# A convolution stage on TensorE: high and low activation parts in one stationary operand, input weights 128 columns wide

## The chip, the cores and the metric

The kernel runs on one core of a Trainium2 chip. The metric is the device time of one execution in microseconds (us). A core has TensorE (PE in the profile, with its weight loads as PEld), VectorE (DVE), ScalarE (ACT), GpSimd (POOL) and SyncE (SP), which here issues nearly all DMAs of the stage under study. The engines run their own queues in order and wait for each other on semaphores.

## The reference

The input x is 16 images of 16 x 16 positions with 192 channels, in float32: 4096 tokens of 192 values. Three layers follow one another. Only the first is touched by the change:

```
xs  = einsum('bhwc,dc->bhwd', x, W1) + b1      # 192 -> 48 channels ("input product")
xs  = gelu(xs)
xs  = |low-pass(xs)|                           # 2-D FFT, mask, inverse FFT, per image and channel
xs  = einsum('bhwd,cd->bhwc', xs, W2) + b2     # 48 -> 192 channels ("output product")
x   = x + xs
```

Then come an attention layer over the 12 heads of each token with a row normalisation ahead of it, and a mixture of 8 experts (top 2) of width 384, each added to x. The result is float32 throughout, and the low-pass is one 256 x 256 matrix over the positions of an image.

## The kernel before, in words

The kernel is four phases, one after the other, each a block of its own that all engines enter and leave together: `conv_phase`, `attention_phase`, `routing_phase`, `expert_phase`. Only `conv_phase` (lines 139 to 436) is touched.

**Tiles.** The 4096 tokens are 32 tiles of 128; four tiles (512 tokens, two images) are one "quad", so there are eight quads. Two slots (`RING` = 2) hold quads in flight; quad number q is 2i + s, in slot s.

**TensorE** does three products for each quad. `in_product` (line 233) takes the transposed x, 192 channels on the partitions in two parts of 128 and 64 (+1 row of ones for the bias), as the stationary operand of 128 tokens, and the 48 columns of W1 as the moving operand, in plain float32: eight products a quad, which the profile shows as 16 matmul instructions (lines 239, 240). `lowpass_product` (line 243) has six: activations split into a high and a low part (`g_hi`, `g_lo`, type float32r), times the 256-wide low-pass matrix, itself split; high x high, high x low and low x high are summed. The two images m of a quad lie at partitions 0 to 63 and 64 to 127, each using 48 rows and one for the bias. `out_product` (line 254) has twelve: for each image m and half h, `yt_hi` x `w2_hi`, `yt_hi` x `w2_lo` and `yt_lo` x `w2_hi`, each on 49 partitions (at 0 or at 64), 192 columns wide. The order on TensorE is written out by hand (lines 268 to 282): in the loop, `in_product(i,0)`, `lowpass_product(i-1,1)`, `out_product(i-1,0)`, `in_product(i,1)`, `lowpass_product(i,0)`, `out_product(i-1,1)`.

**ScalarE** first makes `lp_hi` and `w2_hi` (lines 291 to 295) after five constant loads, and then, per quad, `gelu` (line 297: GELU out of PSUM, and a copy that rounds it to `g_hi`), `magnitude` (line 308: the absolute value twice, into `yt` and rounded into `yt_hi`), and `split` (line 317: rounds one expert's weights, two instructions of 768 columns, waiting for their load).

**VectorE** makes the low parts by subtraction: `g_low` (399), `yt_low` (406), `split` (413, expert weights, `wb_lo`), and `finish` (380: adds the output product to x and takes row statistics).

**GpSimd** makes the other low part of the expert weights (`wa_lo`, line 352) and the four small steps of the row deviation.

**SyncE** issues the loads in one queue, in this order per quad: `load` (the transposed x, after `in_product` of two quads before), `load_rows` (x itself), `load_weights` (line 196: one expert's weights, after `wa_lo` and `wb_lo` of two quads before). So a wait in `load_weights` holds all loads behind it.

Of the kernel before, what the change touches and what calls it, by code (L numbers as in the profile page):

```python
# [138 lines left out]
def conv_phase(nc, xs, shift, rstd, x_tiles, xT, w1, w2, lowpass, wgu, wa_hi, wa_lo, wb_hi, wb_lo, ytab, eye, ident,  # L139
               later):  # L140

    with ExitStack() as stack:
        a = Scope(nc, stack, "conv")
        w1a, w1b = a.sb("w1a", [P, DH]), a.sb("w1b", [CB + 1, DH])
        w2s = a.sb("w2s", [P, C])
# [5 lines left out]
        yt = a.sb("yt", [P, RING, SEQ])  # L151
        yt_hi, yt_lo = a.sb("yt_hi", [P, RING, SEQ], F32R), a.sb("yt_lo", [P, RING, SEQ], F32R)

# [22 lines left out]
        g_lo_done, yt_lo_done = a.sem("g_lo_done"), a.sem("yt_lo_done")  # L176
        g_made = a.sem("g_made")
        pool_turn, dve_turn = a.sem("pool_turn"), a.sem("dve_turn")

        with nc.Block() as block:  # L180
            @block.sync
            def _(sp):
                sp.dma_start(w1a[:], w1[0:P, :]).then_inc(w1_in, 16)
                sp.dma_start(w1b[:], w1[P:C + 1, :]).then_inc(w1_in, 16)

# [19 lines left out]
                load(0, 1)  # L205
                sp.dma_start(lp[:], lowpass.rearrange("(h p) s -> p h s", p=P)).then_inc(consts_in, 16)
                sp.dma_start(w2s[0:DH + 1, :], w2).then_inc(consts_in, 16)
                sp.dma_start(w2s[DP:DP + DH + 1, :], w2).then_inc(consts_in, 16)
# [17 lines left out]
            def _(pe):  # L226
# [6 lines left out]
                def in_product(i, s):  # L233
                    q = quad(i, s)
                    pe.wait_ge(xt_in[s], 32 * i + 32)
                    pe.wait_ge(gelu_done, freed(q))
                    for t in range(QT):
                        at = ps_w1[:, s, t * DH:(t + 1) * DH]
                        nc.tensor.matmul(at, xta[:, s, bass.ts(t, P)], w1a[:], start=True, stop=False)  # L239
                        last = nc.tensor.matmul(at, xtb[:, s, bass.ts(t, P)], w1b[:], start=False, stop=True)  # L240
                    last.then_inc(w1_done, 1)
# [12 lines left out]
                def out_product(i, s):  # L254
                    q = quad(i, s)
                    pe.wait_ge(yt_lo_done, made(q))
                    pe.wait_ge(added, freed(q))
                    for m in range(2):
                        k = slice(DP * m, DP * m + DH + 1)
                        for h in range(2):  # L260
                            at = ps_c[:, s, m, h * C:(h + 1) * C]
                            hi, lo = yt_hi[k, s, bass.ts(h, P)], yt_lo[k, s, bass.ts(h, P)]
                            nc.tensor.matmul(at, hi, w2_hi[k, :], start=True, stop=False)
                            nc.tensor.matmul(at, hi, w2_lo[k, :], start=False, stop=False)
                            last = nc.tensor.matmul(at, lo, w2_hi[k, :], start=False, stop=True)
                    last.then_inc(w2_done, 1)
# [18 lines left out]
            def _(act):  # L285
# [5 lines left out]
                nc.scalar.activation(lp_hi[:], lp[:], ACT.Copy)  # L291
                for k in (0, DP):
                    b = slice(k, k + DH + 1)
                    ins = nc.scalar.activation(w2_hi[b, :], w2s[b, :], ACT.Copy)
                ins.then_inc(const_hi_done, 1)

                def gelu(i, s):
# [4 lines left out]
                    nc.scalar.activation(g[:, s].rearrange("p h m d -> p m h d")[:, :, :, 0:DH],  # L302
                                         ps_w1[:, s, 0:QT * DH].rearrange("p (m h d) -> p m h d", m=2, h=2),
                                         ACT.Gelu).then_inc(g_made, 1)
# [3 lines left out]
                def magnitude(i, s):  # L308
                    q = quad(i, s)
                    act.wait_ge(fft_done, made(q))  # L310
                    act.wait_ge(w2_done, freed(q))
                    act.wait_ge(yt_lo_done, freed(q))
                    for dst in (yt, yt_hi):
                        ins = nc.scalar.activation(dst[:, s, :], ps_f[:, s, 0:SEQ], ACT.Abs, bias=y_bias[:, 0:1])
                    ins.then_inc(abs_done, 1)
# [54 lines left out]
            @block.vector  # L370
            def _(dve):
                nc.vector.memset(xtb[CB:CB + 1, :, :], 1.0).then_inc(bias_row, 1)
                dve.sem_inc(added, RING)
                dve.sem_inc(g_lo_done, RING)
# [18 lines left out]
                nc.vector.tensor_tensor(lp_lo[:], lp[:], lp_hi[:].bitcast(F32), ALU.subtract)  # L393
                for k in (0, DP):
                    b = slice(k, k + DH + 1)
                    ins = nc.vector.tensor_tensor(w2_lo[b, :], w2s[b, :], w2_hi[b, :].bitcast(F32), ALU.subtract)
                ins.then_inc(const_lo_done, 1)

# [7 lines left out]
                def yt_low(i, s):  # L406
                    q = quad(i, s)
                    dve.wait_ge(abs_done, made(q))
                    dve.wait_ge(w2_done, freed(q))
                    nc.vector.tensor_tensor(yt_lo[:, s], yt[:, s], yt_hi[:, s].bitcast(F32),  # L410
                                            ALU.subtract).then_inc(yt_lo_done, 1)

# [975 lines left out]
```

## Time and profile before

| | us |
|---|---|
| median of three runs | 485.05 |
| lowest, highest | 484.86, 489.58 |
| the profiled execution, its own time | 490.49 |
| its span (first to last instruction) | 488.7 |
| TensorE busy in the span | 407.5 (83%) |
| VectorE, ScalarE, GpSimd busy | 273.0, 222.3, 277.1 |
| mean granted TensorE clock that the profile gives | 0.87 |

The convolution stage ends at about 73 us, attention and gate logits take up to about 191 us, routing up to about 232 us, and the experts the rest. Busy time is the time in which an engine has an instruction in it; it tells nothing of how fast the engine is clocked. A timeline row is: start, length, engine, line, operation, what is written and read, the tile's shape, how many instructions were merged in the row, and in brackets how long the engine had stood idle and for whom. The distance between the starts of two rows is the pace of the engine; the length of a matmul is longer, since matmuls overlap.

### The profile page before, as it was taken

Reading aid. Unit: us, or ns where it says so; the run is one execution under the profiler, and the core shown is the slowest. Engines: PE = TensorE matmul, PEld = TensorE weight load, DVE = VectorE, ACT = ScalarE, POOL = GpSimd, SP = SyncE. Lnnn points to the kernel's source line nnn. Section 1 sums busy time; section 2 is a strip of 40 time slices with the busy share of each in tenths; the row PEclk is TensorE's granted clock in tenths of the full one; section 3 lists DMA queues with packets and bytes.
Section 4 is the critical chain, followed back from the end, with each engine's and each line's share of the span. In section 5 each row is a group of like instructions: output and inputs, shape, how many; then the busy total and the mean of one; then the engine's idle time right before and its main releaser. Section 6 shows DMA issues by size and latency. Waiting matters only on the chain.

```text
span 488.7 us, 9018 instructions
## 1 busy us (share of the span) xinstructions
PE 407.5 (83%) x2236; PEld 381.4 (78%) x2237; DVE 273.0 (56%) x716; ACT 222.3 (45%) x513; POOL 277.1 (57%) x297
## 2 busy tenths in 40 slices
PE   5899936886998875175899999999999999999870
PEld 5799925675987674065799999999989989998870
DVE  1266573486677432996356666665555555464540
ACT  3533510435454441084455555555545545555340
POOL 0165560377576540001656787878878788787653
PEclk9999999996595555555799999999999999999895
DMA  7988513003334243100323444444434444444442
GB/s 214 269 202 246 148 14 93 24 1 100 99 101 143 86 122 110 14 0 12 100 40 59 67 71 73 68 68 77 72 63 76 77 60 73 66 75 70 55 42 25
DMA packets 46439, 41.26 MB, mean 84 GB/s; under 512 B 14121, under 2 KB 40524, under 8 KB 46412
## 3 DMA queue, kind: packets, MB, share of 16 engines
q0 software_dynamic: 13824, 16.82, 21.8%
q1 hardware_dynamic: 32588, 24.14, 18.2%
q8 instruction: 10, 0.16, 0.1%
q14 instruction: 17, 0.14, 0.1%
HBM read 25.87 MB, written 15.08 MB: 84 GB/s over the span
## 4 chain that ended last, share of the span: by engine, by line
POOL 20%; issue 15%; DMA 13%; PE 2%; SPq 1%; POOLq 0%; ACT 0%; DVE 0%; ACTq 0%
DMA out<-moe_y,idx_map 13%; POOL moe_xt L1063 10%; POOL out L1071 10%; SPq L1308 1%; DMA moe_xt<-rows,idx_map 1%; POOLq L1056 0%; PE moe_ps_gt L1105 0%; PE moe_ps_x L1096 0%; PE moe_ps_y L1130 0%; PE moe_ps_gt L1106 0%; PE moe_ps_h L1116 0%; PE moe_ps_gt L1107 0%; PE moe_ps_gt L1109 0%; PE moe_ps_u L1105 0%; PE moe_ps_u L1109 0%
## 5 line engine op out<-in xcount | busy, mean ns | idle before, releaser
L1071 POOL DMA_INDIRECT out<-moe_y,idx_map x72 | 114.3, 1587 | 48.0 <-SPq L1319 24.8
L1063 POOL DMA_INDIRECT moe_xt<-rows,idx_map x72 | 71.2, 988 | 58.7 <-issue 58.7
L1206 ACT ACTIVATE moe_yy<-moe_ps_y,moe_xt 128x384 f32<-128x384 f32 x72 | 41.9, 582 | 72.3 <-PE moe_ps_y L1130 72.3
L1130 PE MATMUL moe_ps_y<-wd,moe_h_hi 128*128 x216 | 71.4, 356 | 0.7 <-DVE moe_h_lo L1261 0.5
L1269 DVE TENSOR_TENSOR moe_y<-moe_yy 128x192 f32<-128x192 f32 x72 | 25.9, 359 | 80.2 <-DMA out<-moe_y,idx_map 53.0
L1186 ACT ACTIVATE moe_x_hi<-moe_ps_x 128x256 fp32r<-128x256 f32 x72 | 27.6, 383 | 46.3 <-PE moe_ps_x L1097 46.3
L1130 PEld LDWEIGHTS moe_ps_y<-wd,moe_h_hi 128*128 128x128 f32 x216 | 41.0, 190 | 2.3 <-issue 2.3
L1261 DVE TENSOR_TENSOR moe_h_lo<-moe_ps_h,moe_h_hi 128x384 fp32r<-128x384 f32 x72 | 40.2, 558 | 2.8 <-ACT moe_h_hi L1198 0.5
L1255 DVE TENSOR_TENSOR moe_hid<-moe_ps_u,moe_sg 128x384 f32<-128x384 f32 x72 | 39.5, 549 | 1.2 <-ACT moe_sg L1192 1.2
L1132 PE MATMUL moe_ps_y<-wd,moe_h_lo 128*128 x144 | 36.3, 252 | 0.0
L1116 PE MATMUL moe_ps_h<-eye,moe_hid 128*128 128x128 f32 x216 | 35.8, 275 | 0.0
L1198 ACT ACTIVATE moe_h_hi<-moe_ps_h 128x384 fp32r<-128x384 f32 x72 | 35.4, 492 | 0.7 <-PE moe_ps_h L1116 0.7
L617 PE MATMUL attn_ps_q<-wqa,attn_xa 128*128 128x240 f32 x64 | 27.9, 532 | 9.1 <-ACT attn_xb L649 9.1
L1192 ACT ACTIVATE moe_sg<-moe_ps_gt 128x384 f32<-128x384 f32 x72 | 35.0, 486 | 0.0
L1245 DVE TENSOR_TENSOR moe_x_lo<-moe_ps_x,moe_x_hi 128x128 fp32r<-128x128 f32 x72 | 20.8, 288 | 22.2 <-ACT moe_x_hi L1186 22.0
L1105 PE MATMUL moe_ps_gt<-wa_hi,moe_x_hi 128*128 x72 | 26.5, 368 | 6.5 <-DVE moe_x_hi L1248 6.4
L352 POOL TENSOR_TENSOR wa_lo<-conv_stage,wa_hi 128x768 f32 (+1 forms) x8 | 15.1, 1887 | 28.3 <-ACT wb_hi L320 28.3
L1105 PE MATMUL moe_ps_u<-wa_hi,moe_x_hi 128*128 x72 | 30.9, 429 | 0.0
L617 PEld LDWEIGHTS attn_ps_q<-wqa,attn_xa 128*128 128x128 f32 x64 | 17.2, 283 | 13.9 <-issue 11.7
L1132 PEld LDWEIGHTS moe_ps_y<-wd,moe_h_lo 128*128 128x128 f32 x144 | 27.4, 190 | 0.0
L618 PE MATMUL attn_ps_q<-wqb,attn_xb 65*128 65x240 f32 x64 | 26.6, 510 | 0.0
L239 PE MATMUL conv_ps_w<-conv_w1a,conv_xta 128*128 128x48 f32 x64 | 20.3, 417 | 7.5 <-DMA conv_xtb<-in_xT 7.5
(184 smaller groups left out, 1131.0 us busy)
## 6 DMA issues: line engine op xcount, KB each, us to landing
xs<-in_x SPq DMA_DIRECT2D x8, 384.0 KB, 4.9
conv_stage<-in_wgu SPq DMA_DIRECT2D x8, 384.0 KB, 3.7
conv_stage<-in_wgu SPq DMA_DIRECT2D x16, 192.0 KB, 4.2
rows<-attn_xr SPq DMA_DIRECT2D x8, 384.0 KB, 2.7
out<-xs SPq DMA_DIRECT2D x8, 384.0 KB, 3.4
attn_stage<-in_down SPq DMA_DIRECT2D x8, 288.0 KB, 3.4
conv_xta<-in_xT SPq DMA_DIRECT2D x8, 256.0 KB, 4.1
moe_xt<-rows,idx_map POOLq DMA_INDIRECT x72, 2.8
```

The costliest lines, as they stand in the source:

```text
L617: nc.tensor.matmul(at, xa[:, s, bass.ts(t, P)], wqa[:], start=True, stop=False)
L1063: nc.gpsimd.indirect_dma_start(xt[:, slot, :], None, rows.ap(), bass.IndirectOffsetOnAxis(ap=idx_map[:, j, 0:1], axis=0)).then_inc(gathere ...
L1071: nc.gpsimd.indirect_dma_start(out, bass.IndirectOffsetOnAxis(ap=idx_map[:, j, 1:2], axis=0), y[:, j % YR, :], None, compute_op=ALU.add).t ...
L1105: nc.tensor.matmul(at, x_hi[:, s, 0:P], wa_hi[:, e, w], start=True, stop=False)
L1116: ins = nc.tensor.transpose(ps_h[:, bass.ts(k, P)], hid[:, s, bass.ts(k, P)], eye[:])
L1130: ins = nc.tensor.matmul(both, hi, halves, start=(k == 0), stop=(k == 2))
L1132: nc.tensor.matmul(first, lo, high, start=False, stop=False)
L1192: nc.scalar.activation(sg[:, s, :], ps_g[:, s, 0:HID], ACT.Silu).then_inc(silu_done, 1)
L1198: nc.scalar.activation(h_hi[:, s, :], ps_h[:, 0:HID], ACT.Copy).then_inc(h_hi_done, 1)
L1206: nc.scalar.activation(yy[:, s].rearrange("p h c -> p (h c)"), ps_y[:, s, 0:2 * C], ACT.Copy, scale=xt[:, slot, bass.ds(GC + e, 1)]).then_ ...
L1255: nc.vector.tensor_tensor(hid[:, s, :], ps_u[:, s, 0:HID], sg[:, s, :], ALU.mult).then_inc(hid_done, 1)
L1261: nc.vector.tensor_tensor(h_lo[:, s, :], ps_h[:, 0:HID], h_hi[:, s, :].bitcast(F32), ALU.subtract).then_inc(h_lo_done, 1)
```

## The change

In the input product the weights `w1a`, `w1b` become 128 columns wide, with 80 columns of zeros, so that each matmul moves 128 columns in place of 48 and writes a full 128 columns of PSUM. GELU reads the 48 that count. VectorE fills both tiles with zeros first, and SyncE waits for that (`wide`) before its first load.

In the output product, `yt_hi` and `yt_lo` go into one tile `yt_hl`: for image m, the high part lies on that image's own 64 partitions and the low part on the other 64. With W2's high part on both halves of the partitions, one matmul over 128 partitions gives high x high + low x high, and a second one with W2's low part gives high x low + low x low (a term that was left out before). Twelve matmuls of 49 partitions become eight of 128. ScalarE's magnitude is now three instructions (`yt` on 128 partitions, the high part of each image on 64), and `yt_low` two on 64 partitions. `w2s` is filled with zeros before its load (`w2_filled`), since all 128 partitions are now used; its splits into high and low become one instruction each.

```diff
-        w1a, w1b = a.sb("w1a", [P, DH]), a.sb("w1b", [CB + 1, DH])
+        w1a, w1b = a.sb("w1a", [P, P]), a.sb("w1b", [CB + 1, P])
...
-        yt_hi, yt_lo = a.sb("yt_hi", [P, RING, SEQ], F32R), a.sb("yt_lo", [P, RING, SEQ], F32R)
+        yt_hl = a.sb("yt_hl", [P, RING, 2, SEQ], F32R)
...
             def _(sp):
-                sp.dma_start(w1a[:], w1[0:P, :]).then_inc(w1_in, 16)
-                sp.dma_start(w1b[:], w1[P:C + 1, :]).then_inc(w1_in, 16)
+                sp.wait_ge(wide, 2)
+                sp.dma_start(w1a[:, 0:DH], w1[0:P, :]).then_inc(w1_in, 16)
+                sp.dma_start(w1b[:, 0:DH], w1[P:C + 1, :]).then_inc(w1_in, 16)
...
+                sp.wait_ge(w2_filled, 1)
                 sp.dma_start(w2s[0:DH + 1, :], w2).then_inc(consts_in, 16)
...
-                        at = ps_w1[:, s, t * DH:(t + 1) * DH]
+                        at = ps_w1[:, s, t * P:(t + 1) * P]
...
                     for m in range(2):
-                        k = slice(DP * m, DP * m + DH + 1)
                         for h in range(2):
                             at = ps_c[:, s, m, h * C:(h + 1) * C]
-                            hi, lo = yt_hi[k, s, bass.ts(h, P)], yt_lo[k, s, bass.ts(h, P)]
-                            nc.tensor.matmul(at, hi, w2_hi[k, :], start=True, stop=False)
-                            nc.tensor.matmul(at, hi, w2_lo[k, :], start=False, stop=False)
-                            last = nc.tensor.matmul(at, lo, w2_hi[k, :], start=False, stop=True)
+                            both = yt_hl[:, s, m, bass.ts(h, P)]
+                            nc.tensor.matmul(at, both, w2_hi[:], start=True, stop=False)
+                            last = nc.tensor.matmul(at, both, w2_lo[:], start=False, stop=True)
...
-                for k in (0, DP):
-                    b = slice(k, k + DH + 1)
-                    ins = nc.scalar.activation(w2_hi[b, :], w2s[b, :], ACT.Copy)
-                ins.then_inc(const_hi_done, 1)
+                nc.scalar.activation(w2_hi[:], w2s[:], ACT.Copy).then_inc(const_hi_done, 1)
...
-                    for dst in (yt, yt_hi):
-                        ins = nc.scalar.activation(dst[:, s, :], ps_f[:, s, 0:SEQ], ACT.Abs, bias=y_bias[:, 0:1])
+                    nc.scalar.activation(yt[:, s, :], ps_f[:, s, 0:SEQ], ACT.Abs, bias=y_bias[:, 0:1])
+                    for m in range(2):
+                        b = slice(DP * m, DP * (m + 1))
+                        ins = nc.scalar.activation(yt_hl[b, s, m, :], ps_f[b, s, 0:SEQ], ACT.Abs, bias=y_bias[b, 0:1])
                     ins.then_inc(abs_done, 1)
...
             def _(dve):
+                nc.vector.memset(w1a[:], 0.0).then_inc(wide, 1)
+                nc.vector.memset(w1b[:], 0.0).then_inc(wide, 1)
                 nc.vector.memset(xtb[CB:CB + 1, :, :], 1.0).then_inc(bias_row, 1)
+                nc.vector.memset(w2s[:], 0.0).then_inc(w2_filled, 1)
...
-                    nc.vector.tensor_tensor(yt_lo[:, s], yt[:, s], yt_hi[:, s].bitcast(F32),
-                                            ALU.subtract).then_inc(yt_lo_done, 1)
+                    for m in range(2):
+                        b, o = slice(DP * m, DP * (m + 1)), slice(DP * (1 - m), DP * (2 - m))
+                        ins = nc.vector.tensor_tensor(yt_hl[o, s, m, :], yt[b, s], yt_hl[b, s, m, :].bitcast(F32),
+                                                      ALU.subtract)
+                    ins.then_inc(yt_lo_done, 1)
```

## Rows read from the trace of the kernel before

**Rows 1.** Page, part 2, whole span: granted clock and DMA share in 40 slices.
```profile
PEclk9999999996595555555799999999999999999895
DMA  7988513003334243100323444444434444444442
```

**Rows 2.** Timeline, PE, one quad: start, length, engine, line, operation, count.
```profile
44.96 0.66 PE L239 MATMUL conv_ps_w<-conv_w1a,conv_xta 128*128 128x48 f32 x2
...
48.39 0.56 PE L249 MATMUL conv_ps_f<-conv_lp_hi,conv_g_hi 128*128 128x256 f32 x1
...
49.61 0.41 PE L251 MATMUL conv_ps_f<-conv_lp_hi,conv_g_lo 128*128 128x256 f32 x1
49.95 0.53 PE L263 MATMUL conv_ps_c<-conv_w_hi,conv_yt_hi 49*128 49x192 f32 x1
...
50.50 0.62 PE L263 MATMUL conv_ps_c<-conv_w_hi,conv_yt_hi 49*128 49x192 f32 x2
...
51.68 0.41 PE L265 MATMUL conv_ps_c<-conv_w_hi,conv_yt_lo 49*128 49x192 f32 x1
52.02 0.66 PE L239 MATMUL conv_ps_w<-conv_w1a,conv_xta 128*128 128x48 f32 x2
```

**Rows 3.** Timeline, PE: one kind of instruction (128x128 transpose) at three times.
```profile
85.95 0.42 PE L498 MATMUL attn_ps_b<-eye,attn_xn 128*64 128x128 f32 x1
86.17 0.42 PE L497 MATMUL attn_ps_a<-eye,attn_xn 128*128 128x128 f32 x1
...
103.96 0.27 PE L497 MATMUL attn_ps_a<-eye,attn_xn 128*128 128x128 f32 x1
104.07 0.27 PE L498 MATMUL attn_ps_b<-eye,attn_xn 128*64 128x128 f32 x1
...
129.10 0.42 PE L498 MATMUL attn_ps_rb<-eye,attn_xr 128*64 128x128 f32 x1
```

**Rows 4.** Windows: busy us and count by engine, granted clock, DMA share, GB/s.
```profile
12.00:27.00 15.00, 12.81 (x60) 12.00 (x60) 5.67 (x17) 6.95 (x15) 4.21 (x2) 1.00 1.03 262
27.00:54.00 27.00, 27.00 (x133) 25.43 (x132) 16.10 (x48) 12.20 (x24) 15.58 (x20) 1.00 0.78 213
16.70:52.00 35.30, 35.27 (x170) 33.34 (x170) 18.87 (x55) 15.46 (x31) 18.56 (x21) 1.00 0.86 227
102.30:112.50 10.20, 6.85 (x40) 5.90 (x38) 7.49 (x23) 4.61 (x11) 7.19 (x14) 1.00 0.01 2
112.50:133.00 20.50, 18.40 (x63) 16.00 (x64) 15.70 (x40) 9.65 (x22) 12.29 (x23) 0.50 0.41 119
```

**Rows 5.** Timeline, PE, attention stage: products 240 and 8 columns wide.
```profile
92.24 1.01 PE L617 MATMUL attn_ps_q<-wqa,attn_xa 128*128 128x240 f32 x2
...
103.34 0.57 PE L618 MATMUL attn_ps_q<-wqb,attn_xb 65*128 65x240 f32 x2
...
135.57 0.39 PE L623 MATMUL attn_ps_q<-ga,attn_ra 128*128 128x8 f32 x2
135.89 0.39 PE L624 MATMUL attn_ps_q<-gb,attn_rb 64*128 64x8 f32 x2
```

**Rows 6.** Waits of SP's own queue, 0 to 75 us: total, times, longest.
```profile
SPq L199 <- DVE wb_lo L416: 21.0, 6, 5.1
```

**Rows 7.** Timeline, all engines: start of the kernel, and the second pass.
```profile
0.76 0.40 SPq L183 DMA_DIRECT2D conv_w1a<-in_w  x1
...
1.03 0.91 DVE L372 MEMSET conv_xtb<- 1x1024 f32 x1 [1.03 <-PEq L1380]
...
16.73 0.66 PE L239 MATMUL conv_ps_w<-conv_w1a,conv_xta 128*128 128x48 f32 x2 [1.65 <-DMA conv_xtb<-in_xT]
```

**Rows 8.** Timeline, all engines: splits of one quad; the stage's last instruction.
```profile
43.37 0.47 ACT L314 ACTIVATE conv_yt_hi<-conv_ps_f,conv_y_bias 128x256 fp32r<-128x256 f32 x1
...
43.87 0.43 DVE L410 TENSOR_TENSOR conv_yt_lo<-conv_yt,conv_yt_hi 128x256 fp32r<-128x256 f32 x1 [0.82 <-ACT conv_yt_hi L314]
...
72.54 0.20 POOL L472 TENSOR_TENSOR shift<-conv_minus,rstd 128x4 f32<-128x4 f32 x1 [0.20 <-POOL rstd L467]
```

More of the change, by code:

```diff
@@ L176, in conv_phase @@
         g_lo_done, yt_lo_done = a.sem("g_lo_done"), a.sem("yt_lo_done")
-        g_made = a.sem("g_made")
+        g_made, w2_filled, wide = a.sem("g_made"), a.sem("w2_filled"), a.sem("wide")
         pool_turn, dve_turn = a.sem("pool_turn"), a.sem("dve_turn")
@@ L302, in gelu @@
                     nc.scalar.activation(g[:, s].rearrange("p h m d -> p m h d")[:, :, :, 0:DH],
-                                         ps_w1[:, s, 0:QT * DH].rearrange("p (m h d) -> p m h d", m=2, h=2),
+                                         ps_w1[:, s].rearrange("p (m h d) -> p m h d", m=2, h=2)[:, :, :, 0:DH],
                                          ACT.Gelu).then_inc(g_made, 1)
@@ L393, in _ @@
                 nc.vector.tensor_tensor(lp_lo[:], lp[:], lp_hi[:].bitcast(F32), ALU.subtract)
[L394 to L397, printed above, removed]
+                nc.vector.tensor_tensor(w2_lo[:], w2s[:], w2_hi[:].bitcast(F32),
+                                        ALU.subtract).then_inc(const_lo_done, 1)
                 def g_low(i, s):
```

## The prediction

> **What bounds the kernel now.** I read the page's 40 slices first, then the timeline of one quad, the same instruction at several times to learn the clock, the busy time by stretches, and last the waits of SyncE. In the first slices TensorE is busy without a break and the DMA share is high; the clock digits read 9 throughout the convolution [rows 1]. That digit misleads. A transpose of 128 columns lasts 0.42 us at 85.95, where the page still prints full clock, and 0.27 us at 103.96; it lasts 0.42 us again at 129.10 [rows 3], in a stretch whose granted clock is 0.50 [rows 4]. The spacing is 0.22 us in the first case and 0.11 us in the second [rows 3]. So the printed 1.00 ahead of 102 us is no measurement, and at 85.95 TensorE ran at its lower level, 1.2 GHz.
>
> One quad in the convolution: 16 input matmuls in 48.39 - 44.96 = 3.43 us, 0.214 us each; six low-pass matmuls up to 49.95, 1.56 us; twelve output matmuls up to 52.02, 2.07 us; 7.06 us in all [rows 2]. A slot of 0.214 us is the same for 48 and for 256 moving columns (from 49.61 on, less the gap at the end), and it is the 0.22 us of a transpose at 1.2 GHz: what is paid is the load of 128 stationary columns, at the lower clock. TensorE is busy 35.27 of 35.30 us between 16.7 and 52 [rows 4]. It is the bound there, and DMA is the next one: its share is 1.03 at 262 GB/s in 12 to 27 us, when the second pass of TensorE even waits 1.65 us for x [rows 7], and 0.78 in 27 to 54 us [rows 4].
>
> **The change part by part.**
>
> *Input product, at the lower clock.* The same 16 matmuls, 128 moving columns in place of 48. Bounds: no dearer than now if the weight load stays the limit (0.214 us); at most the 240-wide product, whose pair lasts 1.01 us against the 0.66 us of the 48-wide one [rows 5, 2], so some 0.18 us more each. I take nothing: the nearest row is the transpose, 128 moving columns on 128 stationary ones, and its spacing is 0.22 us [rows 3]. The cover is the weight load; were it gone, 16 x 0.18 = 2.9 us a quad would show.
>
> *Output product, at the lower clock.* Twelve matmuls now take 2.07 us, which is 9.7 slots: the two images lie in different halves of the rows, and a pair of them starts at 50.50 in each other's shadow [rows 2]. Eight of 128 rows can't overlap so: 8 x 0.214 = 1.71 us, plus the gaps at both ends. The gap from 49.61 to 49.95 and that from 51.68 to 52.02 are 0.34 us each, 0.13 over a slot [rows 2]. Between 1.71 and 1.71 + 0.26 = 1.97 us a quad, so 0.10 to 0.36 us saved; I take 0.2, over seven quads on the bound -1.4 us. So a third fewer instructions is worth a tenth of the stage's product, not a third. The Trainium skill, "TensorEngine Tiling (Array Packing)", Key Properties, says that a change of the tiling mode drains TensorE; by it, the gaps at both ends would go with the half-row tiles, and the saving be the upper one, 7 x 0.36 = 2.5 us.
>
> *Start.* SyncE's first load is issued at 0.76 us; VectorE's first instruction is at 1.03 [rows 7]. Now two fills come ahead of the load. The fill of 1024 columns lasts 0.91 us [rows 7], so 128 columns some 0.11 to 0.25 us (below by columns, above with a fixed part): the first load at 1.03 + 2 x 0.17 + 0.1 for the semaphore = 1.5, +0.7 us. Every load stands behind it in SyncE's queue, and TensorE's second pass waits for x [rows 7], so the whole delay counts. The fill of xtb moves behind, to about 2.3 us, under loads that land after 5 us; so does that of w2s. The wait `w2_filled` comes when SyncE has issued eight loads: nothing.
>
> *ScalarE and VectorE.* One more rounding on ScalarE (0.47 us [rows 8], two of 64 partitions in place of one of 128) and one more subtraction on VectorE (0.43 us [rows 8]) per quad. From 27 to 54 us VectorE is busy 16.1 and ScalarE 12.2 of 27 us [rows 4]: hidden under TensorE there. The last two quads have no input product to hide them; the stage's last instruction starts at 72.54 [rows 8] after a chain that runs on VectorE: +0.9 us. The merged splits of W2 save two short instructions at the start, hidden by the wait for x: nothing.
>
> *The clock.* This is the term that decides. TensorE's records show it at 1.2 GHz in the whole convolution although it never rests. It rose in the attention stage in the midst of 240-wide products, and full clock holds from 102.3 to 112.5 [rows 4, 5]. Other such products, as those at 92.24, did not raise it (the pair lasts 1.01 us; 0.57 at 103.34 [rows 5]). In the new form the input product moves 128 columns per slot in place of 48, and the output product works on 128 rows in place of 49: nearer to what TensorE did before it rose, and no row tells whether near enough. The Trainium skill, "TensorE: Matmul & The Clock Gate", Part 1, has a busy TensorE released to the full clock; the trace does not agree that being busy is enough, with 35 us of it at half clock. By the page alone, the change would bring nothing here.
>
> If it rises, a slot costs between 0.11 us (the transposes [rows 3]) and 0.16 us (8-wide products, 0.32 us a pair [rows 5]); a quad has 30 slots, so 3.3 to 4.8 us, plus three gaps of 0.13 us. TensorE then leaves the bound, and DMA takes it: the work of 27 to 54 us is 0.78 x 27 = 21.1 us of share; at the 1.03 of the saturated stretch it takes 20.4 us, 6.6 us less [rows 4]. That is the most. What holds it back is SyncE's wait for `wb_lo`, 21.0 us in six times [rows 6], with the next loads of x queued behind; `wb_lo` comes behind `yt_low` and `finish` on VectorE, so it comes earlier only in part. I take half, -3.5 us (bounds 0 and -6.6). In the tail the last input product and the low-pass and output products shrink by some 3 us of TensorE time, but VectorE is the chain there: -1.5 us (0 to -3). Sum: +0.7 - 3.5 - 1.5 + 0.9 = **-3.4 us**.
>
> **The rivals.**
>
> *A, the clock rises in the convolution for most of the loop:* -3.4 us, its own range -6.5 to -0.5. Chance 0.45.
>
> *B, the clock stays at 1.2 GHz, or rises only while loads are the bound:* +0.7 - 1.4 + 0.9 = +0.2 us. For it: 35 us without a break have not raised it, nor have all stretches of 240-wide products. With both bounds -0.9 to +1.6. Chance 0.30.
>
> *C, the clock rises and the rest follows too:* the whole 6.6 us of DMA and 3 us in the tail: -8.0 us with the start and VectorE counted. Against it: SyncE's waits. Chance 0.10.
>
> *D, slower:* the stage ends at another moment, and attention meets other clock decisions. Full clock from 102.3 to 112.5 covers 6.85 us of TensorE work [rows 4]; at 1.2 GHz this takes 6.85 us more, less what waits hide. I take 5.5 us, so +5.5 us; the spread of the three runs before, 484.86 to 489.58, is of that size. It decides when no 240-wide stretch of that pass raises the clock. Chance 0.15.
>
> **How the numbers follow.** The sum stands against the profiled execution, 490.49 us, which is 5.4 us over the median of 485.05; I take the difference to the median. A: 481.6; B: 485.3; C: 477; D: 490.5. Predicted: 481.6, A's own range 478.5 to 484.5. The range 477.5 to 488.5 takes in A and B with their bounds, leaves out half of C and most of D, under 0.2. This measurement can tell about 1%, 4.85 us. Faster by more: C, and a third of A: 0.26. Slower by more: most of D, 0.13. Within 1%: 0.61.
>
> **What would show it.** Right: spacing of conv matmuls near 0.11 to 0.16 us and a first granted-clock record of 1.00 ahead of 60 us; quads under 6.8 us in the loop; DMA share over 0.9 in 27 to 50 us; SyncE's first load at about 1.5 us; idle time of TensorE in the loop that ends on DMA or VectorE. Wrong: all slots at 0.21 us (then B); input matmuls at 0.3 us or more (the weight load did not cover 128 columns); a twelve-to-eight saving over 0.36 us a quad; the attention stage without full clock (D).

## The result and the profile after

Over 22 runs of each kernel the median is 485.24 us (480.87 to 490.50), and 487.88 us for the kernel before (484.42 to 493.78): ratio 0.9941, 95% interval 0.9914 to 0.9967. Two later comparisons of the same two kernels gave 0.9894 (0.9848 to 0.9940) and 0.9913 (0.9875 to 0.9951). The three ratios put the changed kernel 0.6 to 1.1% under the one before, some 3 to 5 us; the intervals reach from 0.3 to 1.5%. The profiled execution took 490.50 us, span 488.7 us, by chance the same as before; this execution is one of the slow ones, so its total says little and its stages are compared below.

The page's slices of the changed kernel (granted clock, DMA share):

```profile
PEclk9797765679568555555799999999999999999985
DMA  6989602003335341101223444434434444444442
```

The clock digits now move inside the first six slices, where they read 9 before [rows 1]: the records of the clock start at 12.7 us instead of 102.3. The next rows are stretches of the changed kernel (busy us and count of PE, PEld, DVE, ACT, POOL, granted clock, DMA share, GB/s), one at full clock and one at half:

```profile
25.00:30.00 5.00, 3.24 (x29) 3.07 (x28) 4.34 (x14) 4.27 (x9) 2.48 (x2) 1.00 0.91 205
...
50.00:55.00 5.00, 4.28 (x20) 4.29 (x21) 4.01 (x13) 0.82 (x2) 4.03 (x6) 0.53 0.57 168
```

And TensorE's timeline in these two, the same products:

```profile
26.27 0.39 PE L242 MATMUL conv_ps_w<-conv_w1b,conv_xtb 65*128 65x128 f32 x2
...
27.09 0.28 PE L253 MATMUL conv_ps_f<-conv_lp_hi,conv_g_lo 128*128 128x256 f32 x1
27.21 0.25 PE L264 MATMUL conv_ps_c<-conv_w_hi,conv_yt_hl 128*128 128x192 f32 x1
...
27.97 0.27 PE L265 MATMUL conv_ps_c<-conv_w_lo,conv_yt_hl 128*128 128x192 f32 x1
...
53.86 0.63 PE L242 MATMUL conv_ps_w<-conv_w1b,conv_xtb 65*128 65x128 f32 x2
...
55.36 0.41 PE L253 MATMUL conv_ps_f<-conv_lp_hi,conv_g_lo 128*128 128x256 f32 x1
55.57 0.36 PE L264 MATMUL conv_ps_c<-conv_w_hi,conv_yt_hl 128*128 128x192 f32 x1
55.73 0.41 PE L265 MATMUL conv_ps_c<-conv_w_lo,conv_yt_hl 128*128 128x192 f32 x1
...
57.01 0.33 PE L265 MATMUL conv_ps_c<-conv_w_lo,conv_yt_hl 128*128 128x192 f32 x1
```

At full clock the starts of the output product lie (27.97 - 27.21) / 7 = 0.109 us apart, at half clock (57.01 - 55.57) / 7 = 0.206. The pair of input matmuls lasts 0.39 and 0.63 us. The 0.214 us slots of the kernel before were indeed half clock, whatever the page printed there [rows 2 to 4].

Where TensorE's time went is in the waits. The first two rows are from 15 to 60 us, the third from SyncE's queue up to 75 us (us in total, times, longest); the last ones are from the timeline:

```profile
PE conv_ps_w L241 <- DMA conv_xtb<-in_xT: 14.1, 6, 4.6
ACT wa_hi L318 <- DMA conv_stage<-in_wgu: 4.1, 3, 1.9
...
SPq L200 <- DVE wb_lo L419: 19.4, 6, 4.9
...
1.18 0.40 SPq L184 DMA_DIRECT2D conv_w1a<-in_w  x1
...
18.77 0.79 PE L241 MATMUL conv_ps_w<-conv_w1a,conv_xta 128*128 128x128 f32 x2 [4.62 <-DMA conv_xtb<-in_xT]
...
71.53 0.20 POOL L475 TENSOR_TENSOR shift<-conv_minus,rstd 128x4 f32<-128x4 f32 x1 [0.20 <-POOL rstd L470]
```

TensorE waits 14.1 us for x, and 1.65 us before [rows 7]. From 17 to 49 us the DMA share is 0.97, and 0.89 in the kernel before. First the changed kernel, then the one before:

```profile
17.00:49.00 32.00, 22.51 (x150) 21.69 (x150) 19.62 (x57) 17.95 (x36) 17.01 (x18) 0.80 0.97 238
```

```profile
17.00:49.00 32.00, 32.00 (x155) 30.43 (x156) 17.91 (x53) 12.83 (x26) 16.92 (x18) 1.00 0.89 232
```

TensorE now waits for x, so the loads of x, and what delays them, took its place as the bound. It is not the bytes alone: SyncE's wait for `wb_lo` hardly shrank (21.0 to 19.4 us, [rows 6]), and from 29 to 35 us the DMA share is only 0.64, just before TensorE's second-longest wait for x (4.36 us, up to 38.28).

### The profile page after: what moved, and what is told of

Same layout as the page of the kernel before. It is cut to its first block, busy times and chain, and to the rows that moved or that the text cites. A ratio compares the mean times of both kernels' runs of the same rounds, so it can differ in the third digit from the quotient of the medians.

```text
span 488.7 us, 8971 instructions
## 1 busy us (share of the span) xinstructions
PE 384.9 (79%) x2204; PEld 361.2 (74%) x2205; DVE 276.1 (56%) x726; ACT 226.1 (46%) x520; POOL 279.1 (57%) x297
## 4 chain that ended last, share of the span: by engine, by line
POOL 20%; issue 15%; DMA 13%; PE 2%; SPq 1%; DVE 1%; POOLq 0%; another core or an unknown queue 0%; ACT 0%; ACTq 0%; DVEq 0%
DMA out<-moe_y,idx_map 13%; POOL moe_xt L1066 10%; POOL out L1074 10%; SPq L1311 1%; DMA moe_xt<-rows,idx_map 1%; POOLq L1059 0%; PE moe_ps_y L1133 0%; DVE moe_hid L1258 0%; PE moe_ps_x L1099 0%; PE moe_ps_gt L1108 0%; PE moe_ps_u L1112 0%; PE moe_ps_u L1111 0%; DVE moe_x_hi L1251 0%; ACT moe_yy L1209 0%
## 5 line engine op out<-in xcount | busy, mean ns | idle before, releaser
L620 PE MATMUL attn_ps_q<-wqa,attn_xa 128*128 128x240 f32 x64 | 26.7, 510 | 11.7 <-ACT attn_xb L652 11.7
L241 PE MATMUL conv_ps_w<-conv_w1a,conv_xta 128*128 128x128 f32 x64 | 18.2, 380 | 20.1 <-DMA conv_xtb<-in_xT 20.1
L1248 DVE TENSOR_TENSOR moe_x_lo<-moe_ps_x,moe_x_hi 128x128 fp32r<-128x128 f32 x72 | 20.7, 288 | 19.2 <-ACT moe_x_hi L1189 16.1
L241 PEld LDWEIGHTS conv_ps_w<-conv_w1a,conv_xta 128*128 128x128 f32 x64 | 14.4, 277 | 20.8 <-issue 20.8
L1119 PEld LDWEIGHTS moe_ps_h<-eye,moe_hid 128*128 128x128 f32 x216 | 25.8, 141 | 2.7 <-issue 2.2
```

The lines of the kernel that those rows point to most:

```text
L620: nc.tensor.matmul(at, xa[:, s, bass.ts(t, P)], wqa[:], start=True, stop=False)
L1119: ins = nc.tensor.transpose(ps_h[:, bass.ts(k, P)], hid[:, s, bass.ts(k, P)], eye[:])
```

## The experiments

Every profile gives four marks: the start of the third input product (the first that waits for x), the mean of the five periods up to the eighth input product, the start of that one, and the last instruction of the stage (us). "Changed" and "before" were profiled more than once.

| kernel | third | period | eighth | stage end | ratio to before (95%) |
|---|---|---|---|---|---|
| before | 16.73; 17.01 | 7.06; 7.06 | 52.02; 52.31 | 72.54; 72.83 | 1 |
| changed | 18.77; 17.53; 17.66 | 6.39; 6.40; 6.25 | 50.72; 49.51; 48.92 | 71.53; 68.90; 69.56 | 0.9941; 0.9894; 0.9913 |
| wide input alone | 17.29 | 6.51 | 49.83 | 70.47 | 0.9954 (0.9916-0.9993) |
| stacked output alone | 17.21; 17.44 | 6.42; 6.42 | 49.32; 49.52 | 69.13; 70.35 | 0.9948 (0.9906-0.9989); 0.9871 (0.9820-0.9922) |
| changed, 12.5% fewer bytes | 17.86 | 5.74 | 46.58 | 66.66 | 0.9859 (0.9800-0.9919) |
| stacked alone, fewer bytes | 15.56 | 6.23 | 46.72 | 66.55 | 0.9875 (0.9839-0.9912) |
| before, fewer bytes | 16.27 | 7.06 | 51.56 | 72.08 | 0.9932 (0.9900-0.9964) |
| twelve full-row | 17.51 | 7.28 | 53.89 | 75.20 | a single run: 483.51 us |
| eight half-row | 17.72 | 6.14 | 48.40 | 68.14 | a single run: 478.76 us |
| pairs | 16.83 | 6.52 | 49.42 | 69.40 | 0.9930 (0.9893-0.9968) |
| pairs + tail swap | 16.77 | 6.51 | 49.34 | 68.31 | 0.9867 (0.9819-0.9916) |
| stacked + tail swap | 17.49 | 6.47 | 49.85 | 69.99 | 0.9886 (0.9832-0.9941) |
| changed, both ends mended | 17.59; 18.55 | 6.52; 6.35 | 50.21; 50.29 | 69.47; 69.17 | 0.9900 (0.9862-0.9938); 0.9856 (0.9810-0.9901) |

**One part at a time.** Wide input product alone:

> Only the input product's weights are widened to 128 columns; the output product keeps its twelve matmuls on 49 partitions. Theory T (the wide input product alone raises TensorE's clock, loads then bound the loop): granted clock at 1.00 in parts of the convolution, TensorE waits over 10 us for x, eighth input product at about 50.6 us as in the changed kernel (before 52.0), the stage's last instruction at about 71.5 us or 0.9 us less, since VectorE keeps its single subtraction per quad. Rival R1 (it takes the 128 rows of the output product too): no full clock before the attention stage, slots of 0.214 us throughout, eighth input product at 52.5 us, end of stage at 73.0 us.

Stacked output product alone:

> Only the output product is stacked (eight matmuls of 128 partitions); the input product stays 48 columns wide. Theory T: the clock stays at 1.2 GHz in the convolution; a quad takes 0.1 to 0.36 us less than 7.06 us; the eighth input product starts about 1 us earlier (51.0), the tail is 0.4 to 0.9 us longer for the second subtraction, end of stage at 72.0 to 72.5 us, time equal to before within 0.3%. Rival R1 (the rows raise the clock): quads near 6 us that end in waits for x, and a granted clock of 1.00 before 60 us.

The wide input alone does raise the clock: it is granted in full from 11.2 to 18.1 and from 21.5 to 28.3 us. Then it stays low up to the attention stage, and the periods are 5.87, 5.49 and three times 7.06 us. TensorE waits 5.0 us for x, not over 10. So theory T holds in part (the wide input product is enough to raise the clock) and R1 in part (it does not keep it up).

The stacked output alone was the surprise. The first profile has a clock record of 1.00 only from 49.5 us on, yet its periods are 6.51 and four times 6.40 us. Theory T gave at most 0.36 us a quad, and R1 had quads that end in waits for x; neither is what happened, though R1's other sign, a record of 1.00 before 60 us, is there. Its timeline at half clock:

```profile
36.52 0.55 PE L240 MATMUL conv_ps_w<-conv_w1a,conv_xta 128*128 128x48 f32 x2
...
39.84 0.56 PE L250 MATMUL conv_ps_f<-conv_lp_hi,conv_g_hi 128*128 128x256 f32 x1
...
41.06 0.41 PE L252 MATMUL conv_ps_f<-conv_lp_hi,conv_g_lo 128*128 128x256 f32 x1
41.27 0.36 PE L263 MATMUL conv_ps_c<-conv_w_hi,conv_yt_hl 128*128 128x192 f32 x1
...
42.71 0.41 PE L264 MATMUL conv_ps_c<-conv_w_lo,conv_yt_hl 128*128 128x192 f32 x1
42.92 0.34 PE L240 MATMUL conv_ps_w<-conv_w1a,conv_xta 128*128 128x48 f32 x1
```

Input product 3.32 us (3.43 before), low-pass 1.43 (1.56), output 1.65 (2.07) [rows 2]. The product itself gives 0.42 us, and its two neighbours 0.24: the distance into the output product is 41.27 - 41.06 = 0.21, where it was 0.34.

**What the half rows cost.** One run adds a third matmul per half (its result is therefore not the reference's), the other leaves one of three out:

```diff
# twelve full-row (on the stacked kernel)
-                            last = nc.tensor.matmul(at, both, w2_lo[:], start=False, stop=True)
+                            nc.tensor.matmul(at, both, w2_lo[:], start=False, stop=False)
+                            last = nc.tensor.matmul(at, both, w2_hi[:], start=False, stop=True)
# eight half-row (on the kernel before)
-                            nc.tensor.matmul(at, hi, w2_lo[k, :], start=False, stop=False)
```

> The second run's kernel (stacked output product, narrow input product) with a third matmul per half added, the first one repeated, so that there are twelve of 128 partitions again; the sum has the high part of W2 twice. Theory D (the half-row matmuls cost gaps where TensorE changes between them and the full-row products, here gone): a quad takes 6.40 + 4 x 0.214 = 7.25 us at 1.2 GHz, of it 0.34 us less in gaps than in the kernel before, so the stacking's 0.66 us is 4 slots less the overlap of half-row pairs (0.54) plus 0.34 of gaps. Rival S (gaps come from the semaphore waits ahead of each product): the same count of waits stands here, and gaps of 0.34 us between starts would stay at the output product's two ends; they were 0.16 to 0.21 us in the second run, which speaks for D already.

> The kernel before with one of three matmuls of the output product left out (high activations x low weights): eight of 49 partitions in half-row pairs, the same count as in the changed kernel. Theory D (gaps and overlap): the quad falls from 7.06 us by 4 slots less what they overlapped, 3 slots' worth of 0.214 us or less, to about 6.4 to 6.65 us, with gaps of 0.34 us still at both ends of the output product. Rival N (only the number of matmuls matters): 6.40 us as in the second run, and no gap over 0.25 us.

Twelve on all rows: 7.25 us a quad, to the digit. Eight on half rows: 6.10 us, less than either theory gave, with TensorE waiting for x only once, ahead of the third input product, and with all of the loads. Its timeline:

```profile
40.83 0.41 PE L251 MATMUL conv_ps_f<-conv_lp_hi,conv_g_lo 128*128 128x256 f32 x1
41.17 0.54 PE L263 MATMUL conv_ps_c<-conv_w_hi,conv_yt_hi 49*128 49x192 f32 x2
41.50 0.43 PE L264 MATMUL conv_ps_c<-conv_w_hi,conv_yt_lo 49*128 49x192 f32 x2
...
41.92 0.42 PE L264 MATMUL conv_ps_c<-conv_w_hi,conv_yt_lo 49*128 49x192 f32 x2
42.28 0.66 PE L239 MATMUL conv_ps_w<-conv_w1a,conv_xta 128*128 128x48 f32 x2
```

All eight run as four pairs (x2 with hardly more length than one), and the gaps at the two ends, 0.34 and 0.36 us, are there as before. So both halves of theory D are shown: the gaps belong to the change between half-row and full-row products (with full rows in the same order and behind the same semaphore waits they are gone), and half-row neighbours in different halves overlap nearly wholly, 0.21 us from pair to pair. The Trainium skill, "TensorEngine Tiling (Array Packing)", Key Properties, says both, that a change of mode drains the engine and that tiles work independently; the rows agree. In the kernel before, the order of the twelve let only three pairs meet.

Hence the cheapest edit: only the order. For each half and term, image 0 and then image 1:

```diff
-                    for m in range(2):
-                        k = slice(DP * m, DP * m + DH + 1)
-                        for h in range(2):
...
+                    for h in range(2):
+                        for n, (y, w) in enumerate(((yt_hi, w2_hi), (yt_hi, w2_lo), (yt_lo, w2_hi))):
+                            for m in range(2):
+                                k = slice(DP * m, DP * m + DH + 1)
...
```

> The kernel before with the same twelve half-row matmuls of the output product in another order: for each half h and each of the three terms, first image 0 and then image 1, so that neighbours lie in different halves of the rows. Theory D (neighbours in different row halves run as pairs, as all eight did in the sixth run, and only three pairs did in the old order): the output product takes 6 slots and two gaps, 1.74 us in place of 2.07, a quad 6.73 us in place of 7.06, the eighth input product at 50.4 us. Rival N (order does not matter): 7.06 us.

```profile
41.38 0.53 PE L262 MATMUL conv_ps_c<-conv_w_hi,conv_yt_hi 49*128 49x192 f32 x2
...
42.56 0.41 PE L262 MATMUL conv_ps_c<-conv_w_hi,conv_yt_lo 49*128 49x192 f32 x2
42.90 0.67 PE L239 MATMUL conv_ps_w<-conv_w1a,conv_xta 128*128 128x48 f32 x2
```

1.52 us in six pairs, a quad 6.52 us, with no record of full clock before 92 us: better than expected (my sum had counted one slot too many), with no instruction added on any engine.

**Fewer bytes.** Three kernels leave the second copy of 64 rows of expert weights unloaded:

```diff
-                    for k in range(2):
-                        sp.dma_start(stage[k * CB:(k + 1) * CB, s, 1], wgu[P:C, q, :]).then_inc(stage_in[s], 16)
+                    sp.dma_start(stage[0:CB, s, 1], wgu[P:C, q, :]).then_inc(stage_in[s], 16)
```

> The changed kernel with a part of its loads left out: the second copy of the last 64 rows of each expert's gate and up weights is not loaded (that half is filled with zeros once), 192 KB of 1536 KB a quad, 12.5%. Theory T (loads bound the loop once the clock rises): five loop periods shrink from 6.4 us each to about 5.6 to 5.8 us, the eighth input product starts 3 us earlier, TensorE's wait for x shrinks by as much; the end of the stage moves by less, 1 to 3 us, since its tail runs on VectorE. Rival R2 (the order of waits, not the amount loaded, sets the loop, by SyncE's wait for wb_lo): under 1 us in the loop.

> The second run's kernel (stacked output product, input product 48 wide) with the second copy of the 64 rows of expert weights not loaded, as in the third run. Theory T (at 1.2 GHz TensorE and the loads are even at 6.4 us a quad; the wide input product only pays when the loads are shorter): the loop stays at 6.40 us a quad where the clock is low, against 5.7 us in the third run; the eighth input product starts at about 48.5 us against 46.6. Rival R2 (loads alone set the loop): about 5.7 us here too.

> The kernel before with the same part of the loads left out (second copy of 64 rows of expert weights, 12.5% of a quad's bytes). Theory T (TensorE bounds the loop before): 7.06 us a quad to the last digit, eighth input product at 51.3 to 52.0 us, the time within 0.5% of before. Rival R2 (loads bound it already): quads of 6.2 to 6.6 us and a time 0.8% lower.

The kernel before keeps 7.06 us: loads did not bound it. The changed kernel goes from 6.35 to 5.74: the amount loaded counts now, and R2, as priced (under 1 us in the loop), falls. TensorE's wait for x did not shrink by as much as was expected: 10.1 us, against 14.1, 11.6 and 9.7 in the three profiles of the changed kernel. Stacked alone has three periods of 6.4 to 6.5 us, one of 4.28 while its clock was up (22.8 to 33.0 us) and one of 7.50 that ends in a wait of 3.87 us for x; its mean is 6.23. The changed kernel's loop is shorter here, but it starts later (17.86 against 15.56), and the eighth input product, the stage's end and the ratio come out alike: no gain from the wide input is shown even here.

The bytes are not the whole bound, though. The run with eight half-row products loads everything and has a mean period of 6.14 us at 1.2 GHz, where the changed kernel has 6.25 to 6.40; and in it TensorE, which never waits for x in these periods, is what sets them. So the same loads can come faster than the changed kernel gets them. The two differ in the second subtraction on VectorE, ahead of `wb_lo`, and in TensorE's steady pace; which of these delays the loads was not tested. What else stays open: the kernel before with fewer bytes was timed 0.7% faster, while its stage ends only 0.6 us sooner; no stage accounts for the rest.

**Both ends.** The first load of x goes ahead of the wait for the fills, and in the tail:

```diff
                 finish(last, 0)
-                split(last, 1)
                 finish(last, 1)
+                split(last, 1)
```

> The changed kernel with its two ends mended: the first x load is issued before the fills of the weights are waited for, and in the last quads VectorE does the last row statistics ahead of the last wb_lo (nothing in the stage waits for that). Theory T (VectorE is the chain of the tail, 1.25 us of wb_lo stands in it): the stage ends 1.0 to 1.3 us sooner after the eighth input product than in the changed kernel (20.8 and 19.4 us in its two profiles), and the start gives 0.4 us; the time about 0.3% under the changed kernel's. Rival (another engine ends the stage, GpSimd with the row deviation): no gain from the swap.

> Only the stacked output product, without the wide input product, and the same swap at the tail. Theory T2 (at 6.4 us a quad TensorE at 1.2 GHz and the loads are even, so the wide input product brings nothing): eighth input product at 49.0 to 49.5 us, end of stage 1.2 us before the second run's 69.1, so about 68 us, and a time equal to the run beside it (both ends mended, wide input) within 0.4%. Rival W (the wide input product is worth something by itself, as the clock stays up into the tail): the wide one is faster by 0.5% or more.

The tail of the changed kernel (second profile), and that with both ends mended (VectorE and GpSimd):

```profile
62.63 0.38 DVE L457 BATCH_NORM_AGGREGATE conv_mv<-conv_stats 128x2 f32<-128x6 f32 x4 [0.18 <-DVE conv_stats L450]
62.93 1.25 DVE L419 TENSOR_TENSOR wb_lo<-conv_stage,wb_hi 128x768 fp32r<-128x768 f32 x1
...
66.58 0.38 DVE L457 BATCH_NORM_AGGREGATE conv_mv<-conv_stats 128x2 f32<-128x6 f32 x4 [0.18 <-DVE conv_stats L450]
...
67.15 0.23 POOL L466 TENSOR_SCALAR conv_vtmp<-conv_mv 128x4 f32<-128x4 f32 x1 [1.18 <-DVE conv_mv L457]
...
68.90 0.20 POOL L475 TENSOR_TENSOR shift<-conv_minus,rstd 128x4 f32<-128x4 f32 x1 [0.20 <-POOL rstd L470]
```

```profile
63.90 0.38 DVE L457 BATCH_NORM_AGGREGATE conv_mv<-conv_stats 128x2 f32<-128x6 f32 x4 [0.18 <-DVE conv_stats L450]
...
66.65 0.38 DVE L457 BATCH_NORM_AGGREGATE conv_mv<-conv_stats 128x2 f32<-128x6 f32 x4 [0.18 <-DVE conv_stats L450]
66.95 0.92 DVE L419 TENSOR_TENSOR wb_lo<-conv_stage,wb_hi 128x768 fp32r<-128x768 f32 x1
...
67.23 0.74 POOL L466 TENSOR_SCALAR conv_vtmp<-conv_mv 128x4 f32<-128x4 f32 x1 [0.47 <-DVE conv_mv L457]
...
69.47 0.20 POOL L475 TENSOR_TENSOR shift<-conv_minus,rstd 128x4 f32<-128x4 f32 x1 [0.20 <-POOL rstd L470]
```

Between the two aggregates 2.75 us pass in place of 3.95, so the swap does take `wb_lo` off the chain; but GpSimd then needs 2.82 us from the last aggregate to the end and needed 2.32: its first step lasts 0.74 us beside `wb_lo` and 0.23 without it. That is 0.7 us net. From the eighth input product the tail is 19.3 and 18.9 us, against 20.8, 19.4 and 20.6. The stacked kernel with the swap missed its forecast: eighth input product at 49.85 us (49.0 to 49.5 expected), end of stage at 69.99 (about 68), level with the stacked kernel's 69.13 and 70.35. Its last two aggregates are 2.75 us apart too; what it lost lies ahead of them, in the loop and in a tail that varies by more than the 0.7 us.

**Again, side by side.** Four kernels in one comparison, to part what was open:

> The kernel before with the output product's twelve half-row matmuls in pairs and the swap at the tail; no wide input product, no stacking, no further instruction on ScalarE or VectorE. Theory T2 (loads bound the loop at about 6.4 us a quad whatever TensorE does beyond that; the tail is VectorE's): a quad 6.52 us, the stage ends at 68.3 to 68.9 us (69.4 in the run with pairs alone), ratio to before 0.988 to 0.991, no different beyond the intervals from the changed kernel with both ends mended beside it. Rival W (the wide input and the full clock are needed): that one is faster than this by 0.4% or more.

> The changed kernel, unchanged, beside the stacked output product alone on one chip. Theory T2: ratio to before 0.992 within 0.003, equal to that one's within the intervals; in the profile the loop's five periods average 6.4 us and the convolution spends over 20 us at full clock. Rival W: faster than it by 0.4% or more.

> Only the stacked output product, as in the second run, beside the changed kernel on one chip. Theory T2: periods of 6.40 us at 1.2 GHz, the stage ends at 69 to 71 us, the ratio to before equals the changed kernel's within the intervals. Rival W: at least 0.4% slower than it.

> The changed kernel with the start and the tail mended, as in the ninth run, beside the three others on one chip. Theory T: 0.2 to 0.4% faster than the changed kernel beside it (the first load 0.4 us earlier, about 0.7 us less in the tail). Rival: no difference from it.

Ratios 0.9867, 0.9913, 0.9871, 0.9856, each within 0.004 to 0.005. The marks of the stacked kernel missed in one point: the clock was up in its loop too (23.9 to 30.7 us), and its periods are 6.50, 4.70, 7.98, 6.50 and 6.40 us, with the same mean of 6.42. T2 stands in the rest: the full clock (27.3 us of the changed kernel's convolution, 10.2 of the stacked one's, none of the pairs') adds nothing that can be measured, and plain pairs give as much as anything. Rival W (0.4% or more for the wide input) finds no support: over three comparisons the stacked kernel came out 0.5% over the wide one, then 0.1% and 0.4% under it. A difference of some tenths of a per cent either way can't be excluded. The best version of these is the changed kernel with both ends mended by its medians (479.48 and 479.80 us against 483.60 and 486.17), but neither the changed kernel beside it (480.47) nor pairs with the swap (480.83) can be told from it, and the last needs none of the new instructions.

**The unchanged stages.** Two profiles of unchanged kernels:

> The changed kernel, unchanged, for a second profile. Both theories: ratio to before 0.994 within 0.003. Theory T2 (the convolution gives 1 us and the rest of the difference is what attention and the first expert turns get of the clock): the convolution ends within 0.5 us of 71.5 us again, while the lengths of attention and of the first expert turns differ from the first profile by some us in step with the granted clock there. Rival (the stage's own end is what varies): the stage's end differs by over 2 us.

> The kernel before, unchanged, for a second profile. Theory T2: convolution again at 7.06 us a quad and an end at 72 to 73 us, while attention and the experts, untouched by any kernel here, last what the granted clock gives them: attention between 109 and 119 us, shorter the more of it is at full clock, experts 255 to 261 us. Rival (the change itself makes attention shorter): attention at 118 us again, as in the first profile of before.

| profile | attention | of it at full clock | experts |
|---|---|---|---|
| before, first | 118.3 | 23.9 | 256.4 |
| before, second | 110.2 | 47.8 | 255.9 |
| changed, first | 115.7 | 34.1 | 260.0 |
| changed, second | 115.2 | 34.1 | 260.3 |
| changed, third | 110.8 | 44.4 | 256.4 |
| stacked, first | 110.5 | 44.4 | 259.8 |
| fewer bytes, before | 114.4 | 37.5 | 255.9 |

Attention, which no kernel here touches, lasts 108.9 to 118.3 us in 18 profiles, and the experts 255.3 to 260.3. The second profile of the kernel before has one of the three shortest attention stages, and the changed kernel's third has the experts at 256.4 us, as the kernel before. (The experts read over 258 us in the first profile of the changed kernel and in the four of the first comparison after it, and 255.3 to 256.8 in all others; why is open.) So these differences are not the change's, and they are larger than it. They make 3 us unmeasurable in one profile. The rival of the repeat of the changed kernel held: the stage's own end varied by over 2 us (71.5, 68.9 and 69.6), and its ratio, 0.9894, lay just outside the 0.994 within 0.003 that both theories had.

## Why the prediction was right or wrong, point by point

**The base.** The sum was -3.4 us, or -0.7%, and was taken off the median of three runs, 485.05. With 22 runs this median is 487.88; 481.6 us is too low by 3.6 us, of which 2.8 are the base. The change measured 2.6 us between the medians. By the marks the stage ends 2.7 us sooner (70.0 against 72.7 in the means); the loop came out as summed (-3.6 for -3.5), the start 0.4 us dearer than its +0.7, and the tail gave 0.2 where -1.5 + 0.9 = -0.6 was summed. Two slips change no reading: rival B's upper bound follows as +0.9 from its own terms, not +1.6, and SyncE issues seven loads ahead of the wait `w2_filled`, not eight.

**The clock: right that it rises, wrong that it decides.** "This is the term that decides" is the step that failed. It rose in the convolution in every profile of the changed kernel; its slots at full clock are 0.11 us, as bounded. But rival B, the case without it, was priced at +0.2 us, and the runs without it gave nearly the whole gain. The stacked product alone, at 1.2 GHz through the loop in its first profile, ends the stage at 69.13 and 70.35 us, 2.9 us (the means) before the kernel before and level with the changed kernel's mean of 70.0. Pairs, with no full clock in the convolution at all, end it at 69.40. The wrong term behind it is the next one.

**The output product at the lower clock: mis-sized, and the reason for it.** "0.10 to 0.36 us saved; I take 0.2" measured 0.66 us a quad: -3.2 us over the five periods where -1.4 us stood for seven quads. The bound was false because I counted the gaps inside the 2.07 us only. The gap into the product (49.61 to 49.95) lies in the low-pass's 1.56 us, and there was 0.11 more in the input product's 3.43 [rows 2]. I named the rule that tells it, mode changes that drain, and then took its 0.36 from the same wrong sum. The trace of before had shown it: two distances of 0.34 next to slots of 0.214.

**The loop: the number right, by luck in good part.** "I take half, -3.5 us": five periods went from 35.3 us to 31.95, 31.98 and 31.3, -3.6 in the mean. The wait for x took the bound over, as said, at a share of 0.97 where 1.03 was the limit taken. But the half was a guess between two bounds, and the step that was to bring it, the clock, was not needed: stacking alone at half clock gave -3.2. In the changed kernel full clock and waits for x follow each other: the wait of 4.62 us ahead of 18.77 has the clock low from 16.1 to 22.9 us, and the longest period, 7.98 us (7.61 and 7.97 in the other profiles), ends in the wait of 4.36 us in which the clock falls again, at 36.6.

**The start: first load as forecast in kind, its effect larger.** The first load is issued 0.42 us later (0.7 expected); the third input product starts 1.1 us later in the mean of the profiles (18.0 against 16.9). With the load of x put first, it still started at 17.59 and 18.55, so the fills are not shown as the cause; eight half-row products, without fills of the input weights, had it at 17.72. Over all profiles with all of the bytes it lies between 16.73 and 18.77, and what moves it stays open.

**The tail: half wrong.** -1.5 us for TensorE and +0.9 for the added subtractions were expected; the tail went from 20.5 us to 20.3 in the mean. VectorE sets it, as said; its two subtractions last 0.85 us in place of 0.43, and TensorE's speed brought next to nothing there; the three tails of the changed kernel lie 1.4 us apart, so no smaller term can be told.

**Wide input at the lower clock: right.** No dearer: 0.214 us a slot at half clock, periods of 7.06 us in the run with the wide input alone.

**Rival D:** attention does last up to 8 us more or less by the clock it gets, but before and after alike. It is spread, not an effect.

## What to carry to other kernels

Where matmuls on half of the rows stand among full-row ones, look at the distances between starts at both ends, and order them so that neighbours lie in different halves: this order alone was worth as much here, as far as the intervals tell, as stacking, wider operands and a higher clock together. Before buying speed for the engine that is the bound, work out how much it takes for the next one to be the bound; here the changed kernel got 0.7 of 7.06 us before it waited for x, and stacking alone had taken 0.6 of them. Such a limit is not bytes alone: the same loads let another kernel run at 6.10 us. And a stage of 70 us can't be judged by totals that swing by 8 us with the clock of another stage: compare its own marks, in several profiles.

## What was not expected of the hardware

- Ahead of the first clock record the page prints 1.00, but the instructions ran at 1.2 GHz: slots of 0.214 us there, and the same slots where a record says 0.50.
- Eight half-row matmuls took 1.11 us as four pairs, 0.14 us each; eight full-row ones took 1.65 us.
- Entering and leaving half-row products costs 0.13 us each beyond the slot, and the input product behind them lost 0.11 us too: its first step took 0.46 us in the kernel before and 0.35 with the stacked product.
- With 48-wide input and half-row output products (six profiles) no full clock was recorded before 80 us, though TensorE was busy for 35 us without a break in the kernel before. With the wide input (seven profiles) it was there within 13 us of the start; with full-row output products alone (five profiles) at some time from 22.8 to 61.4 us.
- In the changed kernel each fall of the clock up to 52 us came in a wait for x of 1.7 to 4.6 us or within 1.6 us behind it; one wait of 2.06 us, up to 30.30 in the first profile, brought none.
